# State-space loop laid out with eight batches by sixteen states on the partitions

## The reference, cut to what matters

```python
zxBCdt = x @ W_in.T
z, xin, Bm, Cm, dt = jnp.split(zxBCdt, ...)      # 512, 512, 64, 64, 8
xin = jax.nn.silu(conv(xin))                     # 4 taps
xh = xin.reshape(Bsz, L, N_HEADS, HEAD_DIM)      # 8 heads of 64
A = -jnp.exp(A_log)                              # head, channel, state
dt = jax.nn.softplus(dt + dt_bias)               # batch, token, head
def step(h_state, ins):
    x_t, dt_t, B_t, C_t = ins
    a = jnp.exp(dt_t[:, :, None, None] * A[None])
    h_state = a * h_state + B_t[:, None, None, :] * x_t[..., None]
    y_t = jnp.einsum('bhdn,bn->bhd', h_state, C_t)
    return (h_state, y_t)
```

## Time and profile before

| | us |
|---|---|
| median of 3 runs | 1706.47 |
| lowest, highest | 1703.41, 1707.41 |
| the profiled execution's own time | 1700.7 |
| its span | 1699.0 |
| mean granted clock of TensorE (1 is 2.4 GHz) | 0.913 |

### The profile page before, as it was taken

The page is one execution under the profiler, slowest core; times in us unless marked ns, Lnnn a source line. Parts: engine busy times, 40 slices in busy tenths (PEclk is TensorE's granted clock), DMA queues, the critical chain, the costliest instruction groups (busy, mean ns, idle before and its releaser), DMA issues. The chain is left out here.

```text
span 1699.0 us, 32229 instructions
## 1 busy us (share of the span) xinstructions
PE 1476.9 (87%) x11612; PEld 953.0 (56%) x11612; DVE 1417.7 (83%) x1749; ACT 1078.4 (63%) x2662; POOL 1187.8 (70%) x926
## 2 busy tenths in 40 slices
PE   5899999999999998797878887877788687999992
PEld 4688888888888887551111111111111576888882
DVE  4799999999999999866999999999999523666662
ACT  4566666666666665256888888888888123555550
POOL 1878888888888886485999899899899131233323
PEclk9899999999999999988788878888878888999996
DMA  4511111111111110015200000000000014788872
GB/s 121 181 44 35 46 40 47 34 47 40 41 40 47 38 30 1 2 25 150 68 13 12 13 12 12 13 12 14 11 12 8 1 49 181 272 307 314 306 280 84
DMA packets 73023, 127.60 MB, mean 75 GB/s; under 512 B 13410, under 2 KB 60937, under 8 KB 69424
## 3 DMA queue, kind: packets, MB, share of 16 engines
q1 hardware_dynamic: 61168, 55.47, 11.6%
q0 software_dynamic: 9312, 67.90, 11.0%
q10 hardware_dynamic: 2400, 2.36, 0.4%
HBM read 111.03 MB, written 14.68 MB: 74 GB/s over the span
## 5 line engine op out<-in xcount | busy, mean ns | idle before, releaser
L1187 POOL TENSOR_TENSOR expo<-A,dt 128x1024 f32<-128x1024 f32 x189 | 354.5, 1906 | 16.3 <-POOLq L842 15.9
L553 POOL TENSOR_TENSOR half<-prob 128x512 f32<-128x512 f32 (+1 forms) x208 | 266.6, 1282 | 109.2 <-ACT prob L589 107.6
L1298 PE MATMUL ps_y<-state,cz 128*32 128x512 f32 x1024 | 333.1, 738 | 0.8 <-DVE zs L1320 0.8
L1340 DVE TENSOR_TENSOR state<-ps_u,state 128x1024 f32<-128x1024 f32 x252 | 302.8, 1222 | 6.9 <-PE ps_u L1283 0.3
L585 ACT ACTIVATE prob<-ps_s,mx 128x64 f32<-128x64 f32 (+1 forms) x624 | 151.5, 322 | 236.5 <-DVE prob L698 236.5
L693 DVE TENSOR_REDUCE mx<-ps_s 128x16 f32<-128x1024 f32 (+1 forms) x208 | 253.0, 1217 | 15.0 <-PE ps_s L626 11.2
L1231 ACT ACTIVATE direct<-A,dt 128x64 f32<-128x64 f32 x1008 | 258.3, 333 | 0.2
L1219 ACT ACTIVATE ps_a<-expo 128x1024 f32<-128x1024 f32 x189 | 194.2, 1027 | 83.7 <-DVE state L1335 61.3
L1283 PEld LDWEIGHTS ps_u<-x_rows,b_rows 6*64 6x64 bf16 x1024 | 30.5, 106 | 385.3 <-DVE state L1340 251.6
L626 PE MATMUL ps_s<-qbd,kT 64*128 64x256 f32 (+1 forms) x1664 | 216.5, 395 | 24.0 <-ACT prob L585 18.6
L1335 DVE TENSOR_TENSOR state<-ps_a,state 128x1024 f32<-128x1024 f32 x189 | 229.4, 1214 | 0.4 <-ACT ps_a L1219 0.4
(11 more groups left out here) (240 smaller groups left out, 2954.8 us busy)
## 6 DMA issues: line engine op xcount, KB each, us to landing
raw<-in_ctxT_dram SPq DMA_DIRECT2D x80, 268.0 KB, 2.8
raw<-in_ctxT_dram SPq DMA_DIRECT2D x16, 261.0 KB, 2.8
x_slots<-zeros SPq DMA_DIRECT2D x1, 3456.0 KB, 12.3
xg<-x_slots SPq DMA_DIRECT2D x27, 128.0 KB, 4.9
y_slots<-y SPq DMA_DIRECT2D x27, 128.0 KB
ssm_x<-xp ACTq DMA_DIRECT2D x6, 384.0 KB, 4.7
x_rows<-ssm_x SPq DMA_DIRECT2D x96, 24.0 KB
dt<-ssm_dt SPq DMA_DIRECT2D x16, 128.0 KB, 3.6
```

The lines of the kernel that those rows point to most:

```text
L553: pool.tensor_tensor(half[0:rows, :, :], prob[0:rows, g % SLOTS, :, 0:L // 2], prob[0:rows, g % SLOTS, :, L // 2:L], ALU.add).then_inc(hal ...
L1187: pool.tensor_tensor(expo[:, n % EXPS, :, :].rearrange("p a (h c) -> p a h c", h=NH), m["A"][:, :].rearrange("p (h c) -> p h c", h=NH).uns ...
L1298: ins = nc.tensor.matmul(ps_y[Q][32 * j:32 * j + 32, :], m["cz"][:, pair, 32 * tt:32 * tt + 32], state[:, pair, :], start=(tt == 0), stop= ...
L1340: nc.vector.tensor_tensor(h, flat(ps_u[k % 2][:, :, :]), h, ALU.add).then_inc(state_ready, 1)
```

## The change

A partition now holds one of eight batches and one of 16 low states (`BG`, `NLO`); the four high parts of the state (`NHI`) lie in the columns, and the batches are two groups g. The channels are cut in halves hh. A tile is one group and one half: 4 x 256 = 1024 columns; a step still has four, in the order (hh 0: g 0, g 1), (hh 1: g 0, g 1). A pair is the two tiles of one half.

All partitions of one tile have their own batch, so dt can be the scale per partition for every decay: ScalarE makes each tile's decay by four heads, 4 x 64 columns an instruction, and the exponents of GpSimd go. The tiles of g 0 are multiplied by DVE from `ps_a`, those of g 1 by GpSimd; in odd steps GpSimd also multiplies the tile (hh 0, g 0), from `extra`. GpSimd now places C, every four steps.

TensorE makes inputs with a block-diagonal B (`b_diag`: 48 rows of parts and batches, 128 columns), eight matmuls of 256 channels a pair, and outputs with eight matmuls of 256. The order is inputs of pair p, then outputs of pair p - 1. Each `ps_u` belongs to one group, so the inputs of a pair wait for both additions of the pair before; in odd steps, for the first half, the matmuls of g 0 wait only for the addition of g 0.

```diff
         @block.gpsimd
         def _(pool):
-            def exponent(t, q):
...
+            def keep(t, g, hh):
+
+                h = flat(state[:, g, hh, :, :])
+                pool.wait_ge(direct_ready, pool_number(t, g, hh) + 1)
+                pool.wait_ge(y_added, number(t, hh) + 1)
+                pool.tensor_tensor(h, flat(direct[t % 2][:, hh, :, :] if g else extra[:, :, :]), h, ALU.mult)\
+                    .then_inc(pool_kept, 1)
+
+            for i in range(2):
+                place_c(nc, sb, m, i).then_inc(c_placed, 1)
             for t in range(1, L):
-                for q in range(ON_DVE):
-                    if q == 1:
-                        keep(t)
-                    if t + 1 < L:
-                        exponent(t + 1, q)
+                for g, hh in pool_tiles(t):
+                    keep(t, g, hh)
+                if t % 4 == 1 and 4 < t < L - 4:
+                    pool.wait_ge(y_added, 2 * (t - 1))
+                    place_c(nc, sb, m, t // 4 + 1).then_inc(c_placed, 1)
...
+            def pieces(out, t, g, hh):
+                for h in range(NH // 2 * hh, NH // 2 * (hh + 1)):
+                    c = h % (NH // 2) * HD
+                    ins = nc.scalar.activation(out[:, :, c:c + HD], m["A"][:, :, HD * h:HD * (h + 1)], ACT.Exp,
+                                               scale=m["dt"][:, g, NH * t + h:NH * t + h + 1])
+                return ins
...
+            def inputs(pair):
...
+                tiles = [(g, n) for n in range(NHI) for g in range(2)]
+                if t and not on_dve(t, hh):
+                    tiles.sort()
+                    pe.wait_ge(state_ready, 2 * pair - 1)
+                elif pair:
+                    pe.wait_ge(state_ready, 2 * pair)
+                for i, (g, n) in enumerate(tiles):
+                    if t and not on_dve(t, hh) and i == NHI:
+                        pe.wait_ge(state_ready, 2 * pair)
+                    ins = nc.tensor.matmul(ps_u[g][:, n, :], m["b_diag"][rows_of(g), ch % 2, NHI * tt + n, :],
+                                           m["x_rows"][rows_of(g), ch % 2, tt, HALF * hh:HALF * (hh + 1)],
+                                           start=True, stop=True, skip_group_check=True)
...
+            for pair in range(PAIRS + 1):
+                if pair < PAIRS:
+                    inputs(pair)
+                if pair:
+                    outputs(pair - 1)
```

Ahead of the loop, SP clears `b_diag`, `cz` and the bias tile by transfers (2 MB, 1 MB and 0.7 MB), B goes to DRAM in six terms and comes back in 16 transfers of 384 pieces of 32 bytes, C goes the same way, and x rows come in 12 transfers for eight steps. ScalarE issues all stores of x. A's logarithms are loaded during the layer norm ahead. In `ssm_output` four of eight copies of DVE are split in two:

```diff
+            for first, parts in ((0, 3), (3, 2), (5, 1)):
+                for k in range(parts):
+                    sp.dma_start(s["b"][first + k].rearrange("(q b) t n -> (b t) q n", b=2), b3[:, k, :, :])\
+                        .then_inc(b_stored, 16)
...
+            load_b(sp, m, s, 0, b_loaded)
```

More of the change, by code:

```diff
@@ L380, in _ @@
                 act.wait_ge(turned, t + 1)
[L381 to L388, removed]
+                nc.scalar.copy(sb["xlnT"][:, :, t * P:(t + 1) * P],
+                               ps[:, t % 4, 0:KD * P].rearrange("p (c s) -> p c s", c=KD)).then_inc(copied, 1)
 def load_ssm(sp, d, m, loaded):
@@ L802, in rows_loaded @@
[L802 to L814, removed]
@@ L817 @@
[L817 to L825, removed]
-                         s["b0"][:, g::4, :, :].rearrange("k b l n -> k b (l n)")).then_inc(b_loaded[ch], 16)
-        else:
-            for first, parts in ((0, 3), (3, 2), (5, 1)):
-                sp.dma_start(m["b_rows"][row + first:row + first + parts, :, steps, :].rearrange("k b l n -> k b (l n)"),
-                             s["b"][0:parts, ch - 1, g::4, :, :].rearrange("k b l n -> k b (l n)"))\
-                  .then_inc(b_loaded[ch], 16)
@@ new lines, with rows_of @@
+STEP_PARTS = (0, None), (1, 0), (1, 1)
+def rows_of(g):
+    return slice(64 * g, 64 * g + BG * NTERM)
+def load_rows(sp, m, s, i, x_loaded):
+    ch, t = i // 2, i % 2 * TB // 2
+    for g in range(2):
+        turned = (t + g * TB // 2) % TB
+        for part, first, rep in TERMS:
+            for j in range(first, first + rep):
+                row = 64 * g + BG * j
+                sp.dma_start(m["x_rows"][row:row + BG, ch % 2, t:t + TB // 2, :],
+                             s["x"][part, ch, g, turned:turned + TB // 2, :, :].rearrange("t b c -> b t c"))\
+                    .then_inc(x_loaded[2 if i == 1 else ch % 2], 16)
@@ new lines, in outputs @@
+            def outputs(pair):
+                t, hh = pair // 2, pair % 2
+                ch, tt, quad, tm = t // TB, t % TB, t // 4, t % 4
+                pe.wait_ge(state_ready, 2 * pair + 2)
+                if tm == 0 and hh == 0:
+                    pe.wait_ge(c_placed, quad + 1)
+                if tt == 0 and hh == 0 and ch:
+                    pe.wait_ge(y_taken, 2 * ch)
+                for n in range(NHI):
+                    for g in range(2):
+                        col = 32 * ((quad + 2 * g) % 4)
+                        c0 = CZ * tm + 32 * (NHI * g + n)
+                        ins = nc.tensor.matmul(ps_y[g][col:col + 32, HALF * hh:HALF * (hh + 1)],
+                                               m["cz"][:, quad % 2, c0:c0 + 32], state[:, g, hh, n, :],
+                                               start=(tm == 0 and hh == 0 and n == 0), stop=False, skip_group_check=True)
+                ins.then_inc(y_added, 1)
+                if tt == TB - 1 and hh:
+                    for g in range(2):
+                        for c in range(XC):
+                            ins = nc.tensor.matmul(ps_y[g][:, c * P:(c + 1) * P], m["xs"][:, c, tokens_of(2 * ch + g)],
+                                                   m["skip"][:, c, :], start=False, stop=True, skip_group_check=True)
+                        ins.then_inc(y_full, 1)
```

418 lines of the change are left out of this document (191 added, 227 removed).

## The result

The changed kernel takes 1710.68 us, the kernel before 1703.98, each the median of 20 runs on the same chip. The ratio is 1.0036, with a 95% interval of 1.0023 to 1.0049: slower by 6 us, a little more than the 0.3% that was named as what a measurement can tell. The profiled execution has a span of 1705.6 us against 1699.0, 6.6 longer.

What follows compares the result with a forecast made beforehand. DVE was taken to bound the loop before, a chain through TensorE and GpSimd after. Loop +13, ahead of it +5, first step and end +3, stage behind +1: 22 us, so 1728 from 1706.5, range 1684 to 1752.

Steps and rivals of the forecast that it cites:

- The sign: Whole kernel: slower, median from 1706.5 to 1728 us; slower by more than about 5 us was given 0.64.
- the borders: Before, at the ends of and behind the loop: +5 for SP's issuing, +3 first step and end, +1 stage behind.
- The share of half clock: State-space loop: 34% at 1.2 GHz as before, giving 8.63 us a step and 13 us more in 63 steps.
- rival A: Loop: clock stays full because new inputs fill more of the array; 7.99 us a step, 1688 us; chance 0.20.
- rival B: Loop: clock lies between, at 0.90; 8.34 us a step, 1710 us in all; chance 0.12.
- The chain: Even to odd step: additions, inputs, outputs, GpSimd's multiplication, additions take 5.18 us; DVE waits 1.65, then 1.23.
- Output groups: TensorE in the loop: a pair's eight output matmuls take 1.92 us at full clock, 3.66 at half.
- The price of half clock: Loop at half clock: two steps take 20.1 us, one 10.15 with the rest, against 7.99 at full clock.
- C: TensorE's weight loads show in the output groups: 8.92 us a step at mixed clock, 1747 us; chance 0.07.
- D: Loop: TensorE near half clock throughout because it pauses between bursts; 10.15 us a step, 1824 us; chance 0.06.
- E: Ahead of the loop: SP's 16 loads of 32-byte pieces take 20 us more than forecast, 1748 us; chance 0.06.
- F: Loop: GpSimd and its wait not in the way, DVE sets the pace; 6.55 us a step, 1598 us; chance 0.04.

Runs made afterwards that it cites:

- thin inputs: Changed kernel with input matmuls on 8 rows of each operand instead of 48, five of six partial products left out; ratio to the kernel before 1.0162.
- two tiles in every step: Changed kernel with DVE also multiplying the first tile of odd steps, so GpSimd never has a third; ratio to the kernel before 0.9637.
- outputs ahead of inputs: Changed kernel with TensorE issuing the previous pair's outputs before the inputs, only for the second pair of even steps; ratio to the kernel before 0.9983.

## Why the prediction was wrong

The sign was right and the forecast of 22 us was not: it was 6. Two terms were off, in opposite directions, the loop by 28 us and the borders by 13; that they partly cancel is luck, and so is the right sign: the loop, which was to be slower, became faster, and the borders outweighed it.

**The share of half clock.** This step failed: "TensorE's work a step is as before (4 x 1.32 against 2 x 2.42 at full clock), at nearly the same pace; I see no reason for another share." The share was 34% by the clock of 0.83, and it came out at 16% by 0.92. By the same formula, 1 / (0.84/7.99 + 0.16/10.15) is 8.27 us a step; measured were 8.18. The forecast had 8.63 (its own terms give 8.61, a slip of 1 us in all). 63 x 0.36 is 23 us too many in the forecast, and 5 more stand in the rest. The reason against the step stood in the same text, under rival A: the new inputs fill more of the array. With 8 rows instead of 48 the clock is 0.84, and a step 8.56, close to the forecast of 8.63. So the rows account for the clock within the new loop. That they are what changed from before to after is likely and not shown: few rows with short pauses have 0.97, not the 0.83 of before. The outcome is near rival B (clock 0.90, 1710), but B's 1710 is luck: its borders were 13 us too short as well.

**The borders.** Forecast were +9, measured +21.6. TensorE's first inputs start 17.5 later than the 785.3 of before, where +5 was forecast; the other 4.1 are near the forecast 4. In the 17.5:
- The 16 loads into `b_diag` take SP 16.74 us, where 10.2 to 12.5 were forecast: +4.2 to 6.5. The size of one was right (0.73 from start to start for nine of them, forecast 0.64 to 0.78). What was missing is a term for four that take 7.81 together while ScalarE's stores of x are moving; that the stores hold them up is read from this coincidence (what the variants issue there is slow as well: x rows in 7.25 and 9.47 us instead of 4.16), and no run moves the stores.
- The ten stores of b and c take 8.1 us to issue, not 6.4, and land 3.2 after it (767.27 to 770.48), not 1.2: +3.7.
- The last x rows land 10.4 us after their issue, not 2.5: +7.9. This is the largest, and it had no row behind it: the x rows of before had been issued long ahead of the loop, so their landing was never seen.
- Twelve loads of x rows take SP 4.16 us, not 7.7 to 11.8: -3.5 or more. SP's whole list ends at 792.46, within the 786.6 to 793.0 that the forecast's own terms add up to (its 788 is near the low end); the landing is what went beyond them.

The stage behind the loop takes the 24.20 us that it took; +1 was forecast.

**What held.** At full clock two steps take 15.65, forecast 15.75 (7.88 a step). The chain is 5.07, forecast 5.18; waits 1.55 and 1.09, forecast 1.65 and 1.23. Output groups take 1.92 and 3.57, forecast 1.92 and 3.66, so pairing twice today's streaming into a group was right. DVE's busy time in the steady steps is 411 (424 in the whole block), forecast 412; GpSimd waits 138.8 for TensorE, of which 16.7 are the first start, forecast 120. ScalarE's pieces are 0.46 to 0.49 each, and DVE never waits for them. The price of half clock holds at 0.90: with a share of 20%, 15.75 at full clock and 20.1 at half make 16.5 of two steps, measured 16.56. At 0.66 (thin inputs) they make 18.5, and 19.81 are measured, so it was sized too low there.

**The rivals.** A is nearly the truth of single windows (15.65), not of the loop. C does not happen: a group of outputs with its loads takes 1.92 at full clock, as without a charge for loads. The Trainium skill (TensorE: Matmul & The Clock Gate, "The mechanism" of Part 3) has a load overlap running matmuls only where its row group differs, which would have made these groups longer; the 1.92 of the row speaks against it here. D does not happen, but its cause does, in small: the pause in odd steps is followed, in 24 of 31 cases, by one slower group. E does not happen: the loads are 4 to 7 us over the forecast and not 20, and the excess stands where the stores of x move. F does not happen; two tiles in every step brought DVE to set the pace, by leaving it more work.

What stays open: how the fill of the array, TensorE's pauses and whatever else combine to the clock; the four cases fit together, outputs ahead of inputs (0.90 with no pause above 1.7 us) and the kernel before (0.83) do not. And why the x rows land sooner in the other order.

## What to carry to other kernels

Balancing engines by their work in a step is not enough where a step depends on the one before. Moving one multiplication of 1.25 us in two steps from DVE to GpSimd freed DVE on paper, but put 2.37 us into the chain that runs additions, outputs, multiplication, additions, and made waits of 2.64: count the chain through each engine for each assignment before counting busy time. And when a layout changes what stands ahead of a loop, ask of each transfer when it will now land; a landing that was always hidden has no row in the trace.

## What the runs showed of the hardware

TensorE's clock went with how many rows of the array the input matmuls fill, at the same instructions, columns and waits: 48 rows 0.92, 8 rows 0.84 in the odd-even loop, and 1.00 against 0.97 where the pauses are shorter. Twelve transfers of 64 KB into 8 partitions each moved at 66 GB/s with nothing beside them; in an order whose neighbours lie 64 partitions apart they moved at 118 GB/s, against 85 in the same 2.5 us of the old order. A transfer of 384 pieces of 32 bytes costs the queue that issues it 0.73 us from start to start (nine in 6.54), and four took 7.81 while 2.3 MB of stores from the other queue moved at 334 GB/s. Spread over two queues, eight took SP 8.13 us and the other eight, beside them, ScalarE 10.3.
